# Attention maps: a key tile weighed in one piece between its two score bursts

## What is computed

```python
scale = HD ** (-0.5)                                  # HD = 4
q = q.reshape(B, N, H, 2, HD)                         # B, N, H = 2, 1024, 16
k = k.reshape(B, N, H, 2, HD)
v = v.reshape(B, N, H, 2 * HD)
def sdpa(qi, ki):
    s = jnp.einsum('bnhd,bmhd->bhnm', qi, ki) * scale
    p = jax.nn.softmax(s, axis=-1)
    return jnp.einsum('bhnm,bmhe->bhne', p, v)
a1 = sdpa(q[:, :, :, 0], k[:, :, :, 0])
a2 = sdpa(q[:, :, :, 1], k[:, :, :, 1])
o = a1 - lam * a2
```

## Time and profile before

| | us |
|---|---|
| median of three runs | 3578.73 |
| lowest and highest of them | 3574.76, 3584.3 |
| the profiled execution | 3573.86 |
| its span, first to last instruction | 3572.0 |
| stage of the attention maps in it | about 110 to 1009 |

### The profile page before, as it was taken

How to read it: one execution, slowest core, us unless ns; L and a number is a source line. 1 busy time by engine, 2 the same in 40 slices (tenths; PEclk the granted TensorE clock), 3 DMA queues, 4 the chain that set the end, 5 groups by cost and what they waited for, 6 DMA issues and landing times. The chain is left out here.

```text
span 3572.0 us, 70296 instructions
## 1 busy us (share of the span) xinstructions
PE 3145.7 (88%) x27180; PEld 1785.7 (50%) x27180; DVE 2652.9 (74%) x3071; ACT 2004.1 (56%) x2855; POOL 1094.5 (31%) x663
## 2 busy tenths in 40 slices
PE   4899999999975888988888989898888888869997
PEld 3122222222243656565656555565656565548886
DVE  3777777777514989898979897888979797846564
ACT  2466666566622667676666666676767676621111
POOL 1000000000003545455545454544545454500000
PEclk7555755555556999999999999999999999979999
DMA  3000000000001101110111011001101110100001
GB/s 128 16 20 19 20 23 21 19 19 19 11 3 44 48 18 30 56 30 25 30 49 30 24 36 45 28 24 35 50 19 30 36 30 19 29 24 1 0 0 30
DMA packets 68992, 101.97 MB, mean 29 GB/s; under 512 B 28070, under 2 KB 42292, under 8 KB 67892
## 3 DMA queue, kind: packets, MB, share of 16 engines
q1 hardware_dynamic: 67924, 98.35, 9.5%
q10 hardware_dynamic: 864, 0.79, 0.1%
HBM read 36.69 MB, written 7.34 MB: 12 GB/s over the span
## 5 line engine op out<-in xcount | busy, mean ns | idle before, releaser
L858 DVE TENSOR_REDUCE a_minus_max<-a_ps_max 128x1 f32<-128x1024 f32 x512 | 623.3, 1223 | 257.6 <-PE a_ps_max L777 257.0
L757 ACT ACTIVATE a_expT<-a_ps_scoresT 128x512 f32<-128x512 f32 (+1 forms) x683 | 535.0, 809 | 387.8 <-PE a_ps_scoresT L796 387.6
L810 PE MATMUL a_ps_out<-a_expT,v_aug 128*32 128x256 f32 x4096 | 538.4, 619 | 24.4 <-ACT a_outT L746 23.7
L1542 DVE STREAM_TRANSPOSE b_probsT<-b_probs 32x1024 f32<-32x1024 f32 x384 | 474.3, 1235 | 94.3 <-POOL b_probs L1168 85.2
L1144 POOL TENSOR_TENSOR b_turned_q<-b_rot_q,b_turned_q 128x1024 f32<-128x1024 f32 x96 | 226.8, 2363 | 713.6 <-DVE b_turned_q L1476 713.6
L1369 PE MATMUL b_psD<-b_probsT,b_v 128*64 128x128 f32 x3072 | 337.8, 278 | 5.8 <-DVE b_probsT L1542 5.8
L796 PE MATMUL a_ps_scoresT<-a_q_op,a_k_op 26*128 26x512 bf16 x1024 | 333.9, 590 | 6.2 <-ACT a_expT L757 5.6
L1370 PE MATMUL b_psD<-b_probsT,b_v_back 128*64 128x128 f32 x3072 | 332.9, 274 | 0.0
L777 PE MATMUL a_ps_max<-a_k_op,a_q_op 24*128 24x512 bf16 x1024 | 303.0, 589 | 32.5 <-DMA a_k_op<-terms_k 14.4
L1384 PE MATMUL b_psD<-b_w_qkv,b_xs 128*128 (+1 forms) x384 | 211.3, 638 | 110.9 <-ACT b_outT L1233 110.9
L1220 ACT ACTIVATE b_kT<-b_psD 64x512 f32<-64x512 f32 x384 | 227.0, 591 | 143.5 <-PE b_psD L1310 136.5
(11 more groups left out here) (286 smaller groups left out, 5909.2 us busy)
## 6 DMA issues: line engine op xcount, KB each, us to landing
b_v_back<-b_v SPq DMA_DIRECT2D x96, 384.0 KB
b_v_back<-b_v SPq DMA_DIRECT2D x96, 128.0 KB
b_w_qkv<-L_ffn_Wqkv SPq DMA_DIRECT2D x6, 1536.0 KB
a_q_op<-terms_q SPq DMA_DIRECT2D x128, 48.0 KB
a_k_op<-terms_k SPq DMA_DIRECT2D x128, 48.0 KB
joined<-a_outT SPq DMA_DIRECT2D x256, 16.0 KB
b_w_o<-L_ffn_Wo SPq DMA_DIRECT2D x6, 512.0 KB
a_q_op<-a_max_hi SPq DMA_DIRECT2D x128, 2.0 KB
```

The costliest lines, as they stand in the source:

```text
L757: act.activation(expT[:, to:to + 512 * size], ps_scoresT[:, at:at + 512 * size], ACT.Exp, scale=SCALE_A).then_inc(exp_ready, 1)
L810: last_mm = pe.matmul(ps_out[lo:lo + 32, 256 * part:256 * part + 256], v_aug[:, b * T8 + kt, head, :], expT[:, at:at + 256], start=(kt == ...
L858: dve.tensor_reduce(minus_max[p % 2][:, at:at + 1], ps_max[u % 2][:], AX.X, ALU.max, negate=True).then_inc(max_taken, 1)
L1542: dve.transpose(probsT[rows, :, :, rows].rearrange("p c h q -> p h c q"), probs[rows]).then_inc(probsT_ready, 1)
```

## The change

`weigh` loses its `part`. The four matmuls of a key tile take the 512 columns of their blocks at once, and the call stands behind burst A alone. Nothing stands between burst B and burst A of the next key tile. The start flag clears the whole bank width at once, so the flag that let the halves have a group each is not needed.

```diff
-            def weigh(p, kt, part):
+            def weigh(p, kt):
...
-                if part == 0:
-                    pe.wait_ge(exp_ready, exp_of(n + 3) + 1)
-                    if kt == 0 and p >= 1:
-                        pe.wait_ge(out_held, p)
+                pe.wait_ge(exp_ready, exp_of(n + 3) + 1)
+                if kt == 0 and p >= 1:
+                    pe.wait_ge(out_held, p)
                 for place, (side, half) in enumerate(((1, 0), (1, 1), (0, 0), (0, 1))):
                     lo = group(side, half)
-                    at = 512 * ((n + place) % SLOTS) + 256 * part
-                    last_mm = pe.matmul(ps_out[lo:lo + 32, 256 * part:256 * part + 256], v_aug[:, b * T8 + kt, head, :], expT[:, at:at + 256],
-                                        start=(kt == 0 and part == 0), stop=(kt == T8 - 1), skip_group_check=True)
-                if part == 1:
-                    last_mm.then_inc(pv_done, 1)
+                    at = 512 * ((n + place) % SLOTS)
+                    last_mm = pe.matmul(ps_out[lo:lo + 32, :], v_aug[:, b * T8 + kt, head, :], expT[:, at:at + 512],
+                                        start=(kt == 0), stop=(kt == T8 - 1))
+                last_mm.then_inc(pv_done, 1)
...
                     scores(p, kt, 1, 0)
                     if kt >= 2:
-                        weigh(p, kt - 2, 0)
+                        weigh(p, kt - 2)
                     elif p >= 1:
-                        weigh(p - 1, T8 - 2 + kt, 0)
+                        weigh(p - 1, T8 - 2 + kt)
                     if u < UNITS * PAIRS_A:
                         max_scores_of(u + 1)
                     scores(p, kt, 0, 2)
-                    if kt >= 2:
-                        weigh(p, kt - 2, 1)
-                    elif p >= 1:
-                        weigh(p - 1, T8 - 2 + kt, 1)
             for kt in (T8 - 2, T8 - 1):
-                weigh(PAIRS_A - 1, kt, 0)
-                weigh(PAIRS_A - 1, kt, 1)
+                weigh(PAIRS_A - 1, kt)
```

## The result

| | before | after |
|---|---|---|
| median, us | 3581.52 (4 runs) | 3741.64 (4 runs) |
| lowest and highest, us | 3574.76, 3587.58 | 3740.4, 3743.76 |
| profiled span, us | 3572.0 | 3740.9 |
| mean granted clock of the span | 0.844 | 0.822 |

The ratio is 1.0448 with a 95% interval of 1.0427 to 1.0469: the change makes the kernel 4.5% slower. The forecast was 3736 us, in a range of 3700 to 3770.

A forecast was written before the change was run, and what follows sets the result against it. TensorE at the low clock in the attention-map stage was taken as the bound. The profiled 3573.9 us plus 151 for waits and once-a-pair extras plus 11 for the lost high clock gave 3736 us, range 3700 to 3770.

The forecast's parts named there:

- The bound: Attention-map stage: TensorE's own order of work sets the pace at 1.2 GHz, busy 863.8 of about 899 us.
- The wait: Burst A's late score waits for an exponential of burst B's scores in the three-bank ring: 1.33 or 1.75 us from B.
- The weighing: One-piece weighing behind burst A, with the step to the next burst: 1.86 us, against 2.02 for two pieces.
- Once a pair: Per pair of maps (eight key tiles), extra delay at the row of maxima and the output copy: 1.12 us.
- The turn: Transposed row of maxima in burst A waits for VectorE's reduction after burst B: 0.62 us later on the mean.
- the three cases: Key tiles by the exponential waited for: single, 512 wide, 3.73 us; joint, 1024 wide, 4.15 us in the other two.
- the copy of the output: Once per pair of maps, the copy stands behind exponentials and delays its weighing: 0.50 us on the mean.
- The sum: Whole stage: 4.77 us for each of 32 pairs, less 1.3 for two first tiles: 151 us, all showing on TensorE.
- The clock: The 45 us stay at 2.4 GHz would not recur, since tiles never take under 3.73 us: 11.2 us added.
- Rival 1: TensorE's clock rises and stays up in the stage, tiles 2.72 us on the mean: 3420 us; chance 0.06, whole or part.
- Rival 2: Burst-to-weighing switches saved, 0.26 us a tile, 66 us in all, score ring not binding: 3508 us; chance 0.03.
- Rival 3: TensorE takes A's scores up later and runs the weighing ahead of them, no change: 3574 us; chance 0.02.

The follow-up runs named there:

- The two experiments on the exponentials: Changed kernel with one 512-column exponential per score block: 3657.31 us; changed kernel with each exponential taking only 256 columns of each block: 3657.64 us.
- the one on the fourth bank: Changed kernel with 512-column exponentials and half of the maximum scores left out, score ring on four banks against three: 3337.4 us, against 3652.95.
- the two kernels with four banks: Both with 512-column exponentials, half of the maximum scores left out, four score banks: one-piece weighing 3337.4 us, the order before with two halves 3376.84 us.
- exponentials of half the columns: Changed kernel, each exponential taking only the first 256 columns of each block, the other half a constant: 3657.64 us, ratio 1.0249.
- The kernel with short exponentials: Kernel before (two weighing halves) with one 512-column exponential per score block in place of joint 1024 and single 512: 3345.61 us, ratio 0.9378.

## Why the prediction was right

**The bound.** TensorE at the low clock set the pace, and the waits put into its list lengthened the stage one to one. What the stage lost is the 168.9 us of the span to within 1 us.

**The wait.** Predicted 1.33 us from B to A's last score in one case and 1.75 in two; measured 1.34, 1.76 (706.82 to 708.58) and 1.80 (702.62 to 704.42). In the last the exponential began 0.72 us after B, not 0.67; why, no row shows. Tiles: predicted 3.73, 4.15 and 4.15, measured 3.74, 4.16 and 4.20; the mean 4.03 in place of 4.01. The two experiments on the exponentials and the one on the fourth bank show that this wait is the cause, and not only that it is there.

**The weighing.** Predicted 1.86 us, measured 1.87 (704.95 to 706.82). The switches were reckoned at 0.26 us a tile, and the two kernels with four banks have 0.27 between them at the low clock. The Trainium skill says, in TensorEngine Tiling (Tiling Modes, Key Properties), that changing the tiling mode drains the engine. The 0.27 us agree with it. They didn't decide this change.

**Once a pair.** Predicted 1.12 us extra. Three pairs measured 33.96 + 33.56 + 32.6 = 100.1, or 33.4 each, less eight tiles of 4.03: 1.1. The two parts can be told apart by the starts of the weighings in the trace of after. The turn adds 0.92, 0.47 and 0.45 us over the three cases, where 0.90, 0.48 and 0.48 were worked out, and the copy of the output adds 0.97, 0.53 and 0.05, where it was 0.94, 0.52 and 0.03. So this term was right in its parts too.

**The sum.** A pair is 4.94 us longer than the 28.43 of before, where 4.77 were predicted. That is 158 us, less 1.3, and with the 11.2 of the lost high clock it makes 168. The prediction had 162; 5 of the 6 us between them are the 0.02 us a tile.

**The clock.** No rise came, as forecast: the profile has 0.50 over the whole stage, and the four runs have a mean clock of 0.820 to 0.822. But the reason that the prediction gave doesn't hold, so this term, 11 of the 168 us, was right by luck as much as by reasoning. The prediction pointed at three bursts 1.56 us apart ahead of the one rise. Three bursts of the same distance stand in the same trace at nine other places, and no rise follows. One of them:

```profile
505.07 0.61 PE L777 MATMUL a_ps_max<-a_k_op,a_q_op 24*128 24x512 bf16 x2
...
506.63 0.60 PE L777 MATMUL a_ps_max<-a_k_op,a_q_op 24*128 24x512 bf16 x2
...
508.18 0.61 PE L777 MATMUL a_ps_max<-a_k_op,a_q_op 24*128 24x512 bf16 x2
```

It also argued that tiles of 3.73 us can't raise the clock when tiles of 3.37 mostly didn't. The changed kernel with short exponentials has tiles of 3.73 us and its clock rose twice. What makes the clock rise in this kernel stays open.

The kernel before also varies more than I had granted: over its eighteen runs it took from 3505.91 to 3587.58 us, while the changed kernel took 3740.4 to 3743.76. I priced one stay of 45 us, as in the profile that I had. The lower runs have the higher clock: the mean over the span is 0.884 in the run of 3505.91 us and 0.838 in the one of 3586.63, taken on the same chip. So more or longer stays at the high clock go with the lower times, though no profile of such a run shows them one by one. Against the fastest run the change costs 236 us.

**The rivals.** Rival 1, a clock that goes up and stays up (3420 us), didn't come. The clock did rise in the changed order once a fourth bank and short exponentials (with half of the maximum scores left out) had brought the tile down to 2.83 us, but it didn't stay up. Rival 2, the switches (3508 us), failed where the prediction said that it would be decided: an exponential of B's scores began 0.68 to 0.72 us after B in the tiles shown, when A's were due after 0.43. Its saving is real, 0.27 us a tile, but here a wait of 0.90 us or more takes its place. Rival 3, no change at all, failed too: TensorE stood before A's scores in every tile and took nothing from behind them.

## What to carry to other kernels

Work that stands between two producers on an engine also hides what their consumer does. Before two bursts are made neighbours, count the buffers between them and their reader, and the time until the reader frees the first one. The width of the reader's instruction counts there: in this kernel a joint read of two banks (1.02 us) holds the first bank as long as the second, and two short reads can beat one long read although they take more time in sum (1.08 us for two of 512 columns in the kernels with four banks).

## What was not expected of the hardware

Splitting the joint exponential took a wait of 0.2 us out of two bursts in three, and the mean clock of the stage went from 0.53 to 0.88. TensorE's busy share went down from 96% (863.8 of 899 us) to 87% (589.33 of 676 us). Part of that fall only follows from the rise, since the same columns take less time at the high clock. The fair comparison is at the low clock, and there the shares are the same. The kernel with short exponentials, in a stretch just ahead of a rise:

```profile
128.10:138.30 10.20, 9.94 (x80) 2.10 (x80) 7.78 (x8) 7.27 (x15) 0.00 (x0) 0.50 0.17 42
```

That is 97%, and the kernel before was busy for 97% of the 500 us from 400 to 900 and granted 0.50 throughout. So the busy share of the profile didn't tell a stretch before a rise from one without. The Trainium skill, in TensorE: Matmul & The Clock Gate (Why this matters for your kernels), has it that an engine kept busy without gaps gets the full rate. By the busy share of the profile these 500 us speak the other way.

A small saving at the low clock can thus be worth three times its size, or nothing more than itself. The second is the case of exponentials of half the columns: 2.65 us a pair, 85 us by that, 84 measured, and the clock at 0.50 throughout. I can't say beforehand which of the two it will be.
